# Two accumulators in the expert stage, its gating step set ahead of the deferred layer norm, and the first activation load set ahead of the weight loads

## The reference

```python
# attention inside groups of SEG = 4 neighbouring tokens, H = 8 heads of 128, own token masked
qk_in = x @ proj_qk_w.T + proj_qk_b;  v_in = x @ proj_v_w.T + proj_v_b
q = qk_in @ wq.T + bq;  k = qk_in @ wk.T + bk;  v = v_in @ wv.T + bv
attn = softmax(q * scale @ k, diagonal masked);  o = (attn @ v) @ out_proj_w.T + out_proj_b
x1 = layernorm(x + o)
# mixture of experts, E = 8, DFF = 2048, two experts a token (K = 2)
gout = x1 @ Wg.T;  topv, topi = top_k(gout, 2);  comb = one_hot(topi) weighted by softmax(topv)
h = silu(x1 @ W1[e].T + b1[e]) * (x1 @ W2[e].T + b2[e])
out = sum_e comb[:, e] * (h @ W3[e].T + b3[e])
result = layernorm(x1 + out)
```

## Time and profile before

| | us |
|---|---|
| median of 3 runs | 8152.6 |
| lowest and highest of the runs | 7638.82 and 8394.15 |
| the profiled execution | 7637.5 |
| its span on the slowest core, from the first instruction to the last | 7636.0 |
| spans of the eight cores in it | 7602.4 to 7636.0 |

### The profile page before, as it was taken

The page is one execution under the profiler, slowest core; times in us unless marked ns, Lnnn a source line. Parts: engine busy times, 40 slices in busy tenths (PEclk is TensorE's granted clock), DMA queues, the critical chain, the costliest instruction groups (busy, mean ns, idle before and its releaser), DMA issues.

```text
span 7636.0 us, 77038 instructions; the slowest of 8 cores (7602.4 to 7636.0 us)
## 1 busy us (share of the span) xinstructions
PE 6382.0 (84%) x29024; PEld 2825.4 (37%) x29024; DVE 2023.2 (26%) x3464; ACT 1153.7 (15%) x1848; POOL 316.3 (4%) x599
## 2 busy tenths in 40 slices
PE   4666666438999999679999985999999849999995
PEld 1222222113444444234444442344444324444442
DVE  0544444522222222222222222222222222222222
ACT  1222222111111111211111112111111121111111
POOL 0000000000000000000000000000000000000000
PEclk9888888769999999889999997999999979999997
DMA  4111111133443434423333343343344333334441
GB/s 81 39 34 34 34 33 28 38 76 61 73 76 72 78 67 80 87 65 75 75 72 67 68 101 83 61 75 67 67 82 84 75 83 67 67 69 88 76 77 53
DMA packets 145302, 512.76 MB, mean 67 GB/s; under 512 B 45693, under 2 KB 45822, under 8 KB 135978
## 3 DMA queue, kind: packets, MB, share of 16 engines
q0 software_dynamic: 88304, 423.82, 30.1%
q1 hardware_dynamic: 56634, 84.02, 3.6%
HBM read 889.49 MB, written 41.94 MB: 122 GB/s over the span
## 4 chain that ended last, share of the span: by engine, by line
PE 75%; DVE 10%; DMA 6%; ACT 4%; issue 3%; another core or an unknown queue 1%; DVEq 1%; SPq 0%; ACTq 0%; POOLq 0%
PE pm L877 24%; PE pm L810 22%; PE pm L835 21%; DMA w1f<-w1T 4%; PE pb L334 3%; DVE ob L452 2%; PE pb L489 2%; PE pb L369 2%; DMA x1g<-x1f 2%; DVE hsb L845 1%; DVE ob L449 1%; DVEq L117 1%; DMA x1T<-x1t 1%; DVE acc L763 1%
## 5 line engine op out<-in xcount | busy, mean ns | idle before, releaser
L810 PE MATMUL pm<-x1T,w1f 128*128 128x512 bf16 x8192 | 1864.2, 381 | 36.5 <-DMA w1f<-w1T 32.3
L877 PE MATMUL pm<-w3sb,hsb 128*128 128x512 bf16 x8192 | 1807.2, 384 | 64.9 <-DVE hsb L845 62.1
L835 PE MATMUL pm<-x1T,w2f 128*128 128x512 bf16 x8192 | 1851.6, 379 | 0.0
L845 DVE SCALAR_TENSOR_TENSOR hsb<-pm,b2c_s,su 128x512 bf16<-128x512 f32 x1024 | 768.8, 751 | 2834.0 <-PE pm L810 2476.4
L821 ACT ACTIVATE su<-pm,b1c_s 128x512 bf16<-128x512 f32 x1024 | 703.6, 687 | 4318.6 <-PE pm L810 4206.9
L877 PEld LDWEIGHTS pm<-w3sb,hsb 128*128 128x128 bf16 x8192 | 807.7, 99 | 1066.0 <-issue 127.2
L810 PEld LDWEIGHTS pm<-x1T,w1f 128*128 128x128 bf16 x8192 | 800.4, 98 | 1024.1 <-issue 78.6
L835 PEld LDWEIGHTS pm<-x1T,w2f 128*128 128x128 bf16 x8192 | 801.6, 98 | 966.5
L890 DVE SCALAR_TENSOR_TENSOR acc<-pm,comb,acc 128x512 f32<-128x512 f32 x512 | 384.5, 751 | 1460.5 <-PE pm L877 1452.4
L162 POOL DMA_DIRECT2D w1f<-w1T x256 | 135.3, 529 | 3985.3 <-DVE hsb L845 3400.5
L755 PE MATMUL pm<-b3s_s,combT 8*128 8x512 bf16 x64 | 31.7, 595 | 297.8 <-DVE combT L747 297.8
(11 more groups left out here) (94 smaller groups left out, 1823.9 us busy)
## 6 DMA issues: line engine op xcount, KB each, us to landing
w1f<-w1T POOLq DMA_DIRECT2D x256, 512.0 KB, 5.2
w2f<-w2T POOLq DMA_DIRECT2D x256, 512.0 KB, 7.2
w3sb<-w3T POOLq DMA_DIRECT2D x64, 2048.0 KB, 21.7
xres<-x SPq DMA_DIRECT2D x32, 512.0 KB, 4.7
x1f<-ob SPq DMA_DIRECT2D x32, 512.0 KB, 2.6
x1g<-x1f SPq DMA_DIRECT2D x32, 512.0 KB, 4.0
out<-outg SPq DMA_DIRECT2D x32, 512.0 KB, 2.9
Xbf<-x POOLq DMA_DIRECT2D x8, 1024.0 KB, 8.4
```

Source lines behind the costliest of these rows:

```text
L810: return t.matmul(gb[:, :], w1f[sl % 2][:, kt * 256 + off: kt * 256 + off + 128], x1T[:, kt * MCH + half * 512: kt * MCH + half * 512 + 51 ...
L835: return t.matmul(vb[:, :], w2f[sl % 2][:, kt * 256 + off: kt * 256 + off + 128], x1T[:, kt * MCH + half * 512: kt * MCH + half * 512 + 51 ...
L845: return v.scalar_tensor_tensor(hsb[:, f * MCH + half * 512: f * MCH + half * 512 + 512], vb[:, :], b2c[:, e * 16 + f: e * 16 + f + 1], su ...
L877: return t.matmul(bk[:, :], hsb[:, f * MCH + j * 128: f * MCH + j * 128 + 128], w3sb[:, f * D + half * 512: f * D + half * 512 + 512], sta ...
```

## The change

Three edits. First, the load of `Xbf` for chunk 0 is issued on GpSimd's queue ahead of the six weight loads in place of behind them. Second, the accumulator is doubled: chunk `k` uses `acc2[k % 2]`, and the waits on `accg` are gone. Third, at `e == 0` `emit_gating_part2` is emitted ahead of the put-off layer norm in place of behind it. Nothing else of the order of operations is touched, and no operation is added or left out. The second accumulator takes 32 KB more of each partition in the expert stage.

```diff
-    aw = []
-    for wi, (dst, src_) in enumerate(((qkwT, qkwT_h), (vwT, vwT_h),
-                                      (wqT, wqT_h), (wkT, wkT_h),
-                                      (wvT, wvT_h), (opT, opT_h))):
-        aw.append(dma("gpsimd", dst[:, :], src_, sem=ld_aw[wi]))
-
     Xbf = sba("Xbf", [128, 4 * D], BF16)
...
+    xsrc0 = bass.AP(x_h.tensor, 0, [[D, 128], [128 * D, 4], [1, D]])
+    t_xl0 = dma("gpsimd", Xbf[:, :], xsrc0, sem=ld_X)
+    aw = []
+    for wi, (dst, src_) in enumerate(((qkwT, qkwT_h), (vwT, vwT_h),
+                                      (wqT, wqT_h), (wkT, wkT_h),
+                                      (wvT, wvT_h), (opT, opT_h))):
+        aw.append(dma("gpsimd", dst[:, :], src_, sem=ld_aw[wi]))
+
...
     def emit_X1(c):
-        xsrc = bass.AP(x_h.tensor, c * ACH * D, [[D, 128], [128 * D, 4], [1, D]])
-        t_xl = dma("gpsimd", Xbf[:, :], xsrc, deps=take("Xbf"), sem=ld_X)
+        if c == 0:
+            t_xl = t_xl0
+        else:
+            xsrc = bass.AP(x_h.tensor, c * ACH * D,
+                           [[D, 128], [128 * D, 4], [1, D]])
+            t_xl = dma("gpsimd", Xbf[:, :], xsrc, deps=take("Xbf"), sem=ld_X)
...
-    acc = sbm("acc", [128, 8 * D], F32)
+    acc2 = [sbm(f"acc{p}", [128, 8 * D], F32) for p in range(2)]
...
-            t_xr = vop(lambda v, s, j=j, par=par: v.tensor_tensor(
-                xr2[par][:, :], x1g[par][:, :], acc[:, j * D:(j + 1) * D],
-                OP.add),
+            t_xr = vop(lambda v, s, j=j, par=par, k=k: v.tensor_tensor(
+                xr2[par][:, :], x1g[par][:, :],
+                acc2[k % 2][:, j * D:(j + 1) * D], OP.add),
                 [t_xg, acc_tok[(j, 0)], acc_tok[(j, 1)]] + take(f"xr2{par}"))
             use(f"x1g{par}", t_xr)
-            use(f"accg{j}0", t_xr)
-            use(f"accg{j}1", t_xr)
...
-                    def fai(v, s, j=j, half=half):
+                    def fai(v, s, j=j, half=half, k=k):
                         return v.tensor_copy(
-                            acc[:, j * D + half * 512: j * D + half * 512 + 512],
+                            acc2[k % 2][:, j * D + half * 512:
+                                        j * D + half * 512 + 512],
                             pm[half][:, :])
-                    t_ai = vop(fai, [tmm2] + take(f"accg{j}{half}"))
+                    t_ai = vop(fai, [tmm2])
...
             if e == 0:
+                emit_gating_part2()
                 while pend_LN2:
                     pend_LN2.pop(0)()
-                emit_gating_part2()
...
-                    def fac(v, s, j=j, e=e, half=half, bk=bk):
-                        sl_ = acc[:, j * D + half * 512: j * D + half * 512 + 512]
+                    def fac(v, s, j=j, e=e, half=half, bk=bk, k=k):
+                        sl_ = acc2[k % 2][:, j * D + half * 512:
+                                          j * D + half * 512 + 512]
```

## The result

| | us |
|---|---|
| changed kernel, median of 10 runs | 8084.11 |
| lowest and highest | 7532.3 and 8636.77 |
| kernel before, median of 10 runs | 7737.98 |
| lowest and highest | 7633.47 and 8431.71 |
| changed kernel, profiled execution | 7536.16 |

Executions of either kernel come undisturbed (7532 to 7545 us for the changed one) or with some cores at a lower clock and up to 15% longer, so the medians say how many of which were drawn, and only the ratio compares the kernels.

The account below looks back on a forecast made before the run. TensorE, busy 84% of the span, was taken as the bound, so only its idle time could move the time. Savings of 59 + 37 + 1 = 97 us off 7637.5 gave 7540, range 7500 to 7610.

Parts of the forecast that it names:

- The sum: Whole kernel: savings of 59 + 37 + 1 = 97 us off the profiled 7637.5, giving 7540; the forecast had 77%.
- the term for how executions differ: Range of the whole time: eight cores of one execution lie 33.6 us apart, so 30 added at the low end.
- the third rival: Expert stage: closing idle time makes the chip grant less clock; 7810 at a clock of 0.93; chance 5%.
- The estimate of 1090 us more: Expert stage, clock at 13/16 throughout by the skill's limiter rule: 1090 us more, for the kernel before as for this one.
- Every step: Start: loads land in queue order; L334 with qkwT at 28.0, k block 65.3, first v block 77.3, second transposes 123.
- The restart: First v block, after 8 us of idle time waiting for wvT: a cold start at the low clock costs 2.4 us.
- The saving at the start: Attention stage: first v block at 77.3 in place of 137.7, 60.4 us less a restart, taken as 59.
- The mechanism: Chunk boundaries: 64 matmuls run ahead, then the down projection waits near 70 us for the accumulation, three times.
- The terms: Three chunk boundaries: head start of four groups gains 12.3 us each, 37 in all; upper end 14.7 and 44.
- that term: Layer norm at the boundaries: starting later shortens its x1g waits, a gain of 1 us for the three.
- The banks as the end of the head start: Down projection at a boundary: four banks for 16 groups, filled in 16.2 us, then TensorE stops.
- The first rival: Chunk boundaries: layer norm hidden whole, all of 3 x 86 us go, time 7320; chance 10%.

Follow-up runs that it names:

- acc2_only: Kernel before with only the accumulator doubled, loads and layer norm in the old order; no ratio, core 6 took 7601.5 us against 7602.4 for the fastest core before.
- zero_act: Changed kernel with x1T zero-filled and L850 multiplying with b2, so the expert stage computes on zeros, same instructions kept; eight times, 7573.31 to 7824.64 us.
- ln_spread: Changed kernel with the put-off layer norm cut into four stages, one per step f of experts 1 and 2, x1g loaded ahead of the store; 0.9551 of the kernel before.

## Why the prediction was right and where it was wrong

**The forecast of the time and its range.** The sum was 7540; the profiled execution took 7536.16, and the ratio gives 7538; 1.3% was forecast and 1.3% measured. The median of the runs, 8084.11, lies 474 us above the end of the range. The step that failed is the term for how executions differ, in the prediction's paragraph on how the numbers follow: I sized it by the spans of the eight cores of one execution, 33.6 us apart, and added 30 at the low end and nothing at the high end, although the three times shown for the kernel before were 7638.82, 8152.6 and 8394.15. Behind it stands the sentence on the limiter under the third rival. There I took the 0.98 in one stretch of one execution for a bound on the clock in all executions, gave a lower clock 5%, and set aside the 13/16 of the Trainium skill (TensorE: Matmul & The Clock Gate, Part 1) because it disagreed with that one row.

What the runs showed in its place: six of the ten executions had cores at a lower clock, one at 7671.37 and five at 8496.86 to 8636.77. In the longest, the mean clock of all four cores of one die was 0.785 to 0.786, and that of the other die's 0.92. The rows of `acc2_only` show such a clock from within: 0.81, close to 13/16 = 0.8125, held by a core for 1000 us on end while others kept 0.99. The estimate of 1090 us more, for that clock all through the expert stage, had no chance of its own in the prediction, and it is close to what the longest executions took: 8636.77 is 1101 us above the profiled 7536.16. There is no trace of one of these, so that the expert stage ran at 0.81 from end to end there is argued from the time and the mean clock, not shown.

What that rival claimed, that closing gaps makes the chip grant less, is not borne out: the profiled execution of the changed kernel keeps 0.98 to 1.00 on all eight cores in the expert stage, and the kernel before loses its clock too (up to 8431.71 beside this kernel, up to 8762.84 later). Whether the change makes such executions more frequent or deeper stays open; side by side the changed kernel had six of ten, five of them near 8500 or above, and the kernel before five of ten, from 7834 to 8432. A range for the median would have had to reach from 7500 to about 8600. The agreement with 7540 is one between executions in which no core lost its clock, and it was a forecast for such an execution only.

By the Trainium skill (TensorE: Matmul & The Clock Gate, Part 1) the limiter follows current, so zero operands do not trip it; `zero_act` agrees for the expert stage. The same section of the Trainium skill lets it act on a whole die, and throughout, once three of its cores run dense matmuls. The four alike cores at 0.785 to 0.786 in the longest execution agree with the whole die; the executions without any loss, and the two cores of a die at 0.81 beside two at 0.99, disagree.

**Edit 1.** Every step held, within 1.1 us. `qkwT` let L340 start at 28.34 (28.0 forecast), the k block at 64.80 (65.3), the first v block at 77.19 (77.3), the second transposes at 124.06 (123). The restart cost 1.7 us of the 2.4. The saving at the start is 59.1 to 60.1 us on the two cores compared, forecast 59.

**Edit 2.** Nothing, as said (`acc2_only`).

**Edit 3.** The mechanism is that of the forecast: stall moved to L882, 64 matmuls ahead, three waits of 70.7 to 72.5 us on cores 2 and 4, forecast as 70. The terms: 12.3 us a boundary, 37 in all; measured 39.0 on average over the cores, 32.1 on core 4, the least. The layer norm did not become shorter by 1 us: on core 4 L663 waited 103.7 us for `x1g` at the three boundaries where L657 had waited 100.8, so that term was 0 or below, within the bounds of the text. The banks as the end of the head start, argued before from four banks and sixteen groups, are now shown by 32, 64 and 128 matmuls.

**The first rival**, 7320 with the layer norm hidden whole, was rightly held apart from this change, and its price was right: the boundaries of `ln_spread` are 219 us shorter than those of the changed kernel, which with the 39 makes the 258 of the rival. It needed the work cut up, not moved.

## What to carry to other kernels

Where an engine takes its list in order, a put-off block of work that others must wait behind is a stall at either place tried here; moving it gave only the head start that the free buffers allowed (about 3.4 us for each PSUM bank), while cutting it into stages, each due a step later, took it off the boundaries altogether. When several loads wait in one queue, put the one first whose work is needed before the others can be used, and then order the work by the landings. And before giving a range for a time, look at how far apart the times shown lie: a profile is one execution.

## What the runs showed of the hardware

The granted clock of two of a die's four cores fell to 0.81 in the last part of an execution (`acc2_only`, 6500 to 7500 us) in which the other six stayed at 0.99, with the same instructions and 98 to 99% of TensorE's time busy on all. It did so in three of the traces, each time on the pair of the die whose clock had been the higher in the attention stage. With zeros in the expert stage no time above 7825 us was seen in eight, where twelve of the kernel before had four above 8170. ScalarE's table change of 1.28 us, taken twice for each of 24 tiles, cost nothing that shows once it fell into a gap: the boundaries of `ln_spread` and its steps of 6.91 us are as long as without it. After 8.24 us of idle time TensorE's next block ran at a granted clock of 0.50 at first and took 1.7 us longer for it.
